# Two transformer layers on one core: transposed rows kept as high and low parts, queries by split operands, another order on three queues

## The chip, the cores and the metric

The kernel runs on one core of a Trainium2 chip. The metric is the device time of one execution in microseconds (us). Before the change the median of three runs is 758.07 us (757.8 to 762.49). The profiled execution, from which every row below is taken, took 760.31 us. A core has five engines that run side by side and meet at semaphores: PE (matrix products), DVE (vector), ACT (activation and copies), POOL (vector work and indirect DMAs) and SP (which only issues DMAs). Each takes its instructions in the order of the program.

## What is computed

Two layers over x of 2 x 2048 rows of 256 words. Cut to what matters:

```python
xn = layernorm(x)
q, k, v = xn@Wq+bq, xn@Wk+bk, xn@Wv+bv         # layer 0, 16 heads of 16
q, k = rope(q), rope(k)
score = einsum('blhd,bmhd->bhlm', q, k)/4       # no softmax
attn = einsum('bhlm,bmhd->blhd', score, v) @ Wo + bo
top_vals, top_idx = top_k(xn @ router_w.T, 2)   # 8 experts, 2 per row
ffn  = sum_k softmax(top_vals)_k * (relu(xn @ w1[e_k])**2 @ w2[e_k])
x = x + attn + ffn
xn = layernorm(x)                               # layer 1
x = x + block_attention(xn) + experts_take_their_512_best_rows(xn)
```

Since layer 0 has no softmax, the kernel computes K^T V once for each batch and multiplies the rotated queries by it.

## The kernel before

**Stage A (pairs of tiles, m = 0 to 15).** A tile is 128 rows, a pair 256. SP loads a pair (`load_pair`, L484), DVE takes its moments, ACT normalises it into `a_xn`, a ring of eight pairs (`normal`, L1265), PE transposes it into a bank of PSUM (`transpose_pair`, L732) and multiplies it by the weights of keys, values and router (`values`, `keys`). The first two pairs are multiplied as plain fp32, the others by split operands: a number is kept as a high part (the type fp32r) and a low part, and a product is high x high + low x high + high x low. ACT writes the high part (`high_xT_pair`), DVE the low one (`low_xT_pair`, L1679), both into buffers of two pairs, and ACT copies the plain transposed pair into `xT_all` as well (`copy_xT_pair`, L1283). DVE finds the two best experts of each row (`top`, `choose`) and, after a count on PE (`rank`), the slot of each row in a table in DRAM, `xs0_d` (`place`).

**Scatters.** POOL carries the rows to their slots: `scatter_x(g, k)` (L2255 to L2268) takes pair g and choice k (0 or 1), writes the number of each row behind it in `a_xn` (an IOTA, L2263) and issues two indirect DMAs (L2266). Pair g has four in all. The second choice overwrites the number, so it waits until the DMAs of the first have landed (`sc0_out`). The order is: first choice of g, second choice of g-1, first choice of g+1 and so on. `normal(m)` waits until all four DMAs of pair m-8 have landed.

**Queries.** `project(g)` (L811, eight groups of four tiles) multiplies `xT_all` by the weights of the queries, 8 instructions of 512 columns in the trace for a group. ACT adds the bias and writes them back over `xT_all` (`copy_q`, L1307), in between it writes the high parts of w2 (`high_w2_0`), DVE the low ones. POOL rotates a tile of queries by a table of cosines and sines (`rotate_q`, L2274), which SP loads (`load_tables`, L551 and L553): the table of tile i waits until tile i-2 has been rotated, since there are two buffers.

**Experts of layer 0.** When every scatter has landed, SP loads tiles of sorted rows (`load_rows`, L543 and L545; a ring of four, so tiles 4 and up wait for the transposes of tile t-4). PE transposes two tiles (`transpose_rows(d)`, L887), multiplies them by w1 (`hidden_pair(d)`, L904) and by w2 (`result0`, L939); a few attention tiles (`attend`) lie between. This repeats 28 times for pairs, then for single tiles. Layer 1 follows and is not touched. SP loads its weights (L529, L535: nine DMAs) right after stage A, while the stage of the queries begins.

What sets the order everywhere is the program as written: there is no scheduler.

## Time and profile before

| | |
|---|---|
| median of 3 runs | 758.07 us (757.8 to 762.49) |
| the profiled execution | 760.31 us |
| its span, first to last instruction | 758.6 us |
| PE busy | 705.8 us, 93% |
| POOL busy | 454.6 us, 60% |
| stage A and queries | 0 to 118.3 us |
| PE idle before the first rows of the experts | 9.5 us |
| experts of layer 0 | 127.8 us on |

"Busy" is the time in which an instruction of the engine runs. A wait is shown in brackets behind the instruction that had waited, with the instruction that released it. A chain follows the work back from the last instruction, each piece to what released it. The granted clock of PE (PEclk) is 1.0 at 2.4 GHz and 0.5 at 1.2 GHz. "Landing" is the time from the issue of a DMA to its semaphore.

### The profile page before, as it was taken

To read this page: it belongs to the slowest core of one execution; us is meant where nothing else is said; L and a number is where in the kernel's file an instruction comes from. 1 tells how busy PE (TensorE), PEld (TensorE's weight loads), DVE (VectorE), ACT (ScalarE), POOL (GpSimd) and SP (SyncE) were. 2 spreads that over 40 slices of the span, in tenths; PEclk is the share of its full clock that TensorE was granted. 3 is DMA by queue.
4 is the path that set the end of the run, shared out by engine and by line. 5 is a ranking of instruction groups with operands and counts; after the bars stand their busy time and mean duration, and the time that the engine had idled before them with its cause. 6 is when DMAs were issued, how large, how long until landed. Compare 5 with 4: busy or idle time off the path is not lost.

```text
span 758.6 us, 19586 instructions
## 1 busy us (share of the span) xinstructions
PE 705.8 (93%) x6224; PEld 631.0 (83%) x6224; DVE 560.0 (74%) x1295; ACT 453.2 (60%) x959; POOL 454.6 (60%) x577
## 2 busy tenths in 40 slices
PE   6999995799999999999998999899999899999994
PEld 4999842799999999999977999777778678888883
DVE  4999771587878888788658886599898777676732
ACT  5666482576776677755525888456677664544411
POOL 3677776799788797988422223034376555655363
PEclk9999997999999999999999999799999999999998
DMA  8699573344445344444178985145457755666352
GB/s 240 183 265 328 185 170 99 90 126 115 129 135 143 104 121 140 130 122 115 41 207 264 313 278 172 30 96 123 109 111 187 223 203 134 148 149 149 50 57 28
DMA packets 151106, 113.99 MB, mean 150 GB/s; under 512 B 59359, under 2 KB 141282, under 8 KB 151012
## 3 DMA queue, kind: packets, MB, share of 16 engines
q1 hardware_dynamic: 137812, 86.94, 41.2%
q0 software_dynamic: 12624, 25.35, 13.4%
q8 instruction: 50, 0.82, 0.5%
q10 hardware_dynamic: 576, 0.53, 0.3%
q14 instruction: 44, 0.36, 0.1%
HBM read 68.68 MB, written 40.80 MB: 144 GB/s over the span
## 4 chain that ended last, share of the span: by engine, by line
PE 85%; DVE 6%; issue 3%; ACT 2%; DMA 1%; POOL 1%; SPq 0%; POOLq 0%; ACTq 0%; DVEq 0%
PE banks L939 13%; PE bank L1195 11%; PE bank L904 11%; PE banks L1206 5%; PE bank L995 5%; PE banks L834 4%; PE bank L915 4%; PE bank L1102 3%; PE banks L770 3%; PE bank L1085 3%; PE banks L823 3%; PE banks L1012 3%; PE bank L776 3%; PE bank L1074 2%; PE bank L887 2%
## 5 line engine op out<-in xcount | busy, mean ns | idle before, releaser
L939 PE MATMUL banks<-r_split,rt_split 128*128 x852 | 110.6, 284 | 1.0 <-issue 0.9
L2297 POOL DMA_INDIRECT ults_by_choice_and_token<-rw,y_id x71 | 79.2, 1115 | 46.5 <-ACT rw L1403 36.3
L939 PEld LDWEIGHTS banks<-r_split,rt_split 128*128 128x128 f32 x852 | 104.9, 191 | 1.6 <-issue 1.6
L904 PE MATMUL bank<-wqkv_split,rt_split 128*128 128x256 f32 x560 | 88.5, 290 | 3.9 <-DVE rt_split L1818 3.8
L1195 PE MATMUL bank<-r_split 128*128 128x512 f32 x384 | 89.6, 391 | 1.3 <-issue 1.1
L1195 PEld LDWEIGHTS bank<-r_split 128*128 128x128 f32 x384 | 71.4, 188 | 16.3 <-issue 1.9
L904 PEld LDWEIGHTS bank<-wqkv_split,rt_split 128*128 128x128 f32 x560 | 77.6, 193 | 5.9 <-DVE rt_split L1818 5.7
L2396 POOL DMA_INDIRECT out_x<-r,idx x32 | 50.2, 1569 | 52.9 <-DVE r L2155 45.2
L2266 POOL DMA_INDIRECT rows_by_expert<-rw,slots x64 | 67.2, 1051 | 18.6 <-issue 9.8
L1818 DVE TENSOR_TENSOR rt_split<-r,rt_split 128x512 fp32r<-128x512 f32 x56 | 59.8, 1108 | 20.0 <-ACT rt_split L1326 20.0
L1843 DVE TENSOR_TENSOR rt_split<-rw,rt_split 128x512 fp32r<-128x512 f32 x71 | 62.9, 918 | 7.4 <-ACT rt_split L1396 7.1
L1581 ACT ACTIVATE r<-bank 128x512 f32<-128x512 f32 x32 | 19.2, 599 | 63.6 <-PE bank L1195 63.6
L2324 POOL TENSOR_TENSOR rw<-rw,bo_s 128x512 f32<-128x512 f32 x16 | 20.6, 1290 | 59.1 <-DVE rw L1892 54.1
L1837 DVE TENSOR_TENSOR rw<-rw 128x512 f32<-128x512 f32 x44 | 42.0, 954 | 18.9 <-ACT rw L1385 18.5
L1385 ACT ACTIVATE rw<-bank 128x512 f32<-128x512 f32 x71 | 41.9, 591 | 20.2 <-PE bank L904 12.0
L1396 ACT ACTIVATE rt_split<-rw 128x512 fp32r<-128x512 f32 x71 | 41.3, 618 | 17.6 <-DVE rw L1837 17.6
L1206 PE MATMUL banks<-r_split 128*128 128x256 f32 x384 | 48.4, 285 | 1.5 <-DVE r_split L2145 0.8
L995 PE MATMUL bank<-rt_split,wqkv_split 128*128 128x256 f32 x384 | 49.2, 283 | 0.3 <-ACT r L1460 0.3
L1206 PEld LDWEIGHTS banks<-r_split 128*128 128x128 f32 x384 | 46.7, 192 | 2.4 <-DVE r_split L2145 1.2
L1326 ACT ACTIVATE rt_split<-r 128x512 fp32r x56 | 32.3, 624 | 25.8 <-PE bank L904 25.6
L995 PEld LDWEIGHTS bank<-rt_split,wqkv_split 128*128 128x128 f32 x384 | 46.3, 188 | 0.8 <-issue 0.7
L2354 POOL DMA_INDIRECT r<-rows_layer,idx x32 | 36.7, 1146 | 14.0 <-issue 13.9
(284 smaller groups left out, 1768.2 us busy)
## 6 DMA issues: line engine op xcount, KB each, us to landing
rt<-in_w SPq DMA_DIRECT2D x24, 512.0 KB, 4.7
rw<-rows_by_expert SPq DMA_DIRECT2D x71, 128.0 KB
r<-in_w SPq DMA_DIRECT2D x16, 512.0 KB
rt<-ults_by_choice_and_token SPq DMA_DIRECT2D x32, 256.0 KB, 3.9
rw<-in_x SPq DMA_DIRECT2D x16, 256.0 KB, 4.7
rw<-in_sin_q SPq DMA_DIRECT2D x32, 128.0 KB
rw<-x_layer SPq DMA_DIRECT2D x16, 256.0 KB
x_plus_bias<-rw SPq DMA_DIRECT2D x16, 256.0 KB, 3.2
```

The lines of the kernel that those rows point to most:

```text
L904: last = pe.matmul(bank[1 + b][:, k * 2 * P:(k + 1) * 2 * P], w[:, c, o:o + P], x[d % 2][:, c, :], start=n == 0, stop=n == 3 * DC - 1)
L939: last = pe.matmul(bank[6 + t % 2][:, 0:D], hidden_T(h, t, c), w[:, ds(e2, 1), o + c * D:o + (c + 1) * D], start=n == 0, stop=n == 3 * HC - 1)
L995: last = pe.matmul(bank[banks[b]][:, j % 2 * D:(j % 2 + 1) * D], w[:, c, j * P:(j + 1) * P], x[:, v.k % 2, c, :], start=k == 0, stop=k == ...
L1195: last = pe.matmul(bank[2 * (hb % 2) + k][:, :], w[:, o:o + P], x[:, s.par, c, :], start=n == 0, stop=n == 3 * DC - 1)
L1206: last = pe.matmul(bank[6 + i % 2][:, 0:D], h[:, s.par, c, i * P:(i + 1) * P], w[s.par][:, o:o + D], start=c == 0 and n == 0, stop=c == HC ...
L1385: act.activation(c_r[:, t % 2, :], bank[1 + t % 2][:, :], ACT.Relu).then_inc(relu_sb, 1)
L1818: dve.tensor_tensor(c_w1lo[:, c, :].unsqueeze(1), r1[:, ds(e1, 1), c * H:(c + 1) * H], c_w1hi[:, c, :].unsqueeze(1).bitcast(F32), ALU.subt ...
L1837: dve.tensor_tensor(c_sq[:, t % 2, :], c_r[:, t % 2, :], c_r[:, t % 2, :], ALU.mult).then_inc(sq_r, 1)
L1843: dve.tensor_tensor(c_lo[:, t % XB, :, :].rearrange("p c n -> p (c n)"), c_sq[:, t % 2, :], c_hi[:, t % XB, :, :].rearrange("p c n -> p (c ...
L2266: pool.indirect_dma_start(xs0_d[:, :], bass.IndirectOffsetOnAxis(slots0_v[:, k, GT * g + j:GT * g + j + 1], 0), a_xn[:, g % NX, j, :], Non ...
L2297: pool.indirect_dma_start(y0_d[:, :], bass.IndirectOffsetOnAxis(y_id[:, t:t + 1].bitcast(I32), 0), c_y[:, t % XB, :], None, bounds_check=l ...
L2396: pool.indirect_dma_start(out[:, :], bass.IndirectOffsetOnAxis(idx1[:, e * TE + i:e * TE + i + 1], 0), f_y[s.par][:, i, :], None, bounds_c ...
```

## The change

It has these parts.

1. **High and low for all pairs.** `xT_all` no longer holds the plain transposed rows. ACT writes the high part of every pair into `xhi_all` (in its place) and DVE the low part into `xlo_all` (the memory of w2's high parts). For the first two pairs ACT makes a plain copy besides (`a_raw`). For 14 pairs ACT has one copy less, for two pairs DVE has one subtraction more.
2. **Queries by split operands.** The weights of the queries are loaded at m = 5 and split by ACT (m = 8) and DVE (m = 9). `project` multiplies high and low parts: 12 instructions of 512 columns for a group. The last group is cut in two: its first half stands ahead of `transpose_rows(0)`, its second behind it.
3. **w2's parts later.** w2's high part e takes the place of `xlo_all`'s group e, so it waits for `project(e)`. One is made after each group, and the last behind the last group. ACT makes w1's high part ahead of the first sorted rows.
4. **Numbers ahead of scatters.** The first eight pairs are numbered by one IOTA at the start. The IOTA of the second choice stands between the two DMAs of the next pair's first choice.
5. **SP's queue.** Behind the last scatter SP loads sorted rows 0 to 3 first, then the tables of tiles 2 and 3, of 4 and 5, and then the weights of layer 1 (they take the place of the queries' split weights, so they wait for `q_ps`), and then sorted rows 4.

```diff
@@ SP
-            sp.wait_ge(k_ps, NPR)
-            for dst, src in ((wqkv1_s[:, :, 0:3 * D], wqkv1.rearrange("(c p) n -> p c n", p=P)),
...
+            def load_late_consts():
+                sp.wait_ge(q_ps, NQ)
+                for dst, src in ((wqkv1_s[:, :, 0:3 * D], wqkv1.rearrange("(c p) n -> p c n", p=P)),
...
             sp.wait_ge(zero_out, 16 * (E + 1))
+            for t in range(XB):
+                load_rows(t)
             for i in range(2, 4):
                 load_tables(i)
                 load_xq(i)
-            for t in range(XB):
-                load_rows(t)
             for i in range(4, QE):
                 load_tables(i)
+            load_late_consts()
@@ PE
+                hi, lo = xhi_all[:, :, g * QT * P:(g + 1) * QT * P], xlo_all[:, g, :, :]
+                for r in parts:
+                    if g >= 2:
+                        pe.wait_ge(q_sb, 2 * (g - 2) + r + 1)
+                    n = 0
                     for c in range(DC):
-                        last = pe.matmul(bank[Q_BANKS[g % 2][r]][:, :], wqkv0_s[:, c, KVR + r * P:KVR + (r + 1) * P],
-                                         xT_all[:, c, g * QT * P:(g + 1) * QT * P], start=c == 0, stop=c == DC - 1)
+                        for w, x in ((wq_hi, hi), (wq_hi, lo), (wq_lo, hi)):
+                            last = pe.matmul(bank[Q_BANKS[g % 2][r]][:, :], w[:, c, r * P:(r + 1) * P], x[:, c, :],
+                                             start=n == 0, stop=n == 3 * DC - 1)
+                            n += 1
...
             for g in range(3, NQ):
+                project(g, range(DC if g < NQ - 1 else 1))
                 if g == NQ - 1:
                     transpose_rows(0)
-                project(g)
+                    project(g, range(1, DC))
@@ ACT
             def high_xT_pair(m):
                 act.wait_ge(aT_ps, 2 * (m + 1))
...
+                if m < NF:
+                    act.activation(a_raw[:, m, :, :], both, ACT.Copy).then_inc(xraw_r, 1)
+                act.activation(xhi_all[:, :, 2 * m * P:2 * (m + 1) * P], both, ACT.Copy).then_inc(aT_sb, 2)
...
+            high_w2_0(E - 2)
+            high_w1(0)
+            high_rows_T(0)
+            copy_q(NQ - 1)
+            high_w2_0(E - 1)
@@ DVE
+            for e in range(E - 1):
+                low_w2_0(e)
+            low_w1(0)
             low_rows_T(0)
-            low_w1(0)
+            low_w2_0(E - 1)
@@ POOL
+            first_ids = number_rows(0, 0, NX)
+            for g in range(NG + 1):
+                if g < NG:
+                    if g >= NX:
+                        pool.wait_ge(sc0_out[g % 4], 16 * TOPK * GT * ((g - NX) // 4 + 1))
+                        first_ids = number_rows(g, 0)
                     pool.wait_ge(slot_r, g + 1)
                     if g >= 4:
                         pool.wait_ge(sc0_out[g % 4], 16 * TOPK * GT * (g // 4))
...
+                    pool.wait_ge(pseq, first_ids)
+                    scatter_x(g, 0, 0)
+                if g >= 1:
+                    h = g - 1
+                    pool.wait_ge(sc0_out[h % 4], 16 * TOPK * GT * (h // 4) + 16 * GT)
+                    second_ids = number_rows(h, 1)
                 if g < NG:
-                    scatter_x(g, 0)
+                    scatter_x(g, 0, 1)
                 if g >= 1:
-                    scatter_x(g - 1, 1)
+                    pool.wait_ge(pseq, second_ids)
+                    for j in range(GT):
+                        scatter_x(h, 1, j)
```

Three places show how the instructions now stand.

POOL, in the middle of the scatters (the DMAs write a table in DRAM, `rows_by_expert`; `rows_scattered` is the semaphore of their landing, `pool_chain` that of the IOTA). Before:

```order
L2263 IOTA rw 128x2 [waits rows_scattered_0]
L2266 DMA rows_by_expert<-rw,slots 66432x257 [waits pool_chain]
L2266 DMA rows_by_expert<-rw,slots 66432x257
L2263 IOTA rw 128x2 [waits slots_ready]
L2266 DMA rows_by_expert<-rw,slots 66432x257 [waits pool_chain]
L2266 DMA rows_by_expert<-rw,slots 66432x257
L2263 IOTA rw 128x2 [waits rows_scattered_1]
```

Now:

```order
L2268 IOTA rw 128x2 [waits rows_scattered_2]
L2275 DMA rows_by_expert<-rw,slots 66432x257
L2275 DMA rows_by_expert<-rw,slots 66432x257 [waits pool_chain]
L2275 DMA rows_by_expert<-rw,slots 66432x257
L2275 DMA rows_by_expert<-rw,slots 66432x257 [waits pool_chain,rows_scattered_0,slots_ready]
L2268 IOTA rw 128x2 [waits rows_scattered_3]
L2275 DMA rows_by_expert<-rw,slots 66432x257
```

The IOTA of the second choice waited with four DMAs between it and the last one that it waits for (two of the pair before, two of the next). Now three stand between: two of the second choice of the pair before, one of the next pair's first. The DMAs behind the IOTA no longer wait for it, save the third.

SP, behind the last scatter (`rows_by_expert` to `rw` and `y_id` are a tile of sorted rows and their numbers, `in_cos_q` and `in_sin_q` the table of a tile of queries; `q_products` counts rotated tiles). Before:

```order
L551 DMA rw<-in_cos_q 128x128 [waits tile_table_ready,rows_scattered_3,zero_rows_stored,rows_scattered_2,q_products,rows_scattered_1,rows_scattered_0]
L553 DMA rw<-in_sin_q 128x2x128
L561 DMA rw<-in_x 128x256
L551 DMA rw<-in_cos_q 128x128 [waits q_products]
L553 DMA rw<-in_sin_q 128x2x128
L561 DMA rw<-in_x 128x256
L542 TENSOR_LOAD tile_r
...
L543 DMA rw<-rows_by_expert 128x256
...
L545 DMA y_id<-rows_by_expert 128x1
L542 TENSOR_LOAD tile_r
```

Now:

```order
L551 DMA rw<-rows_by_expert 128x256
...
L553 DMA y_id<-rows_by_expert 128x1
L559 DMA rw<-in_cos_q 128x128 [waits q_products]
L561 DMA rw<-in_sin_q 128x2x128
L569 DMA rw<-in_x 128x256
...
L559 DMA rw<-in_cos_q 128x128 [waits q_products]
...
L559 DMA rw<-in_cos_q 128x128 [waits q_products]
...
L538 DMA wqkv<-in_wqkv 128x2x768 [waits q_in_psum]
L538 DMA wo_s<-in_wo 128x2x256
...
L544 DMA bv_c<-in_bv 32x2x1 x4
L550 TENSOR_LOAD tile_r [waits rows_loaded_0,rows_T_in_psum]
```

The tables of tiles 2 and 3 stood ahead of the sorted rows and now stand behind them; the nine loads of layer 1's weights (`in_wqkv` to `in_bv`), which stood ahead of the very first tables, now stand between the table of tile 5 and sorted rows 4 (the last row).

PE, around the first sorted rows (`ident,rw` are the transposes of sorted rows; `512`-column products are the queries, `bank` and `banks` their halves). Before:

```order
L887 MATMUL bank<-ident,rw 128x128 [waits ktv_masked,rows_loaded_1,rows_loaded_0]
L887 MATMUL bank<-ident,rw 128x128 x3
L823 MATMUL bank<-r,wqkv 128x512 [waits q_ready]
L823 MATMUL bank<-r,wqkv 128x512
L823 MATMUL banks<-r,wqkv 128x512 x2
L887 MATMUL bank<-ident,rw 128x128 [waits q_ready,rows_loaded_3,rows_loaded_2]
L887 MATMUL bank<-ident,rw 128x128 x3
L904 MATMUL bank<-wqkv_split,rt_split 128x256 [waits rows_T_low_ready,w1_copied,m_ready]
L904 MATMUL bank<-rw_split,rt_split 128x256
```

Now:

```order
L831 MATMUL bank<-r_split,wqkv_split 128x512 [waits q_ready]
L831 MATMUL bank<-r_split,wqkv_split 128x512
L831 MATMUL bank<-r_split,wq_high_or_w_low_split 128x512
...
L897 MATMUL bank<-ident,rw 128x128 [waits ktv_masked,rows_loaded_1,rows_loaded_0]
L897 MATMUL bank<-ident,rw 128x128 x3
L831 MATMUL banks<-r_split,wqkv_split 128x512 [waits q_ready]
L831 MATMUL banks<-r_split,wqkv_split 128x512
L831 MATMUL banks<-r_split,wq_high_or_w_low_split 128x512
...
L897 MATMUL bank<-ident,rw 128x128 [waits q_ready,rows_loaded_3,rows_loaded_2]
L897 MATMUL bank<-ident,rw 128x128 x3
L914 MATMUL bank<-wq_high_or_w_low_split,rt_split 128x256 [waits rows_T_low_ready,w1_copied,m_ready]
```

Half of the last group of queries has moved ahead of the first transposes, and its products read parts instead of plain words.

## Rows read from the trace of the kernel before

**Rows 1.** The page's first lines: the span; busy time, share and instructions of each engine.

```profile
span 758.6 us, 19586 instructions
...
PE 705.8 (93%) x6224; PEld 631.0 (83%) x6224; DVE 560.0 (74%) x1295; ACT 453.2 (60%) x959; POOL 454.6 (60%) x577
```

**Rows 2.** Windows: busy us (instructions) of each engine, PEclk, DMA share, GB/s.

```profile
128.00:130.00 2.00, 2.00 (x6) 1.33 (x6) 0.47 (x1) 0.95 (x2) 0.00 (x0) 0.50 0.37 85
...
142.00:144.00 2.00, 2.00 (x13) 2.00 (x12) 2.00 (x3) 1.11 (x2) 1.96 (x2) 0.58 0.19 55
```

**Rows 3.** Chain that ended last, in order of time: start us, us, what.

```profile
90.60 3.54 PE banks L823 x8
...
127.78 1.09 PE bank L887 x4
128.87 3.38 PE bank L823 x4
132.25 1.73 PE banks L823 x4
...
136.04 2.86 PE bank L904 x24
...
141.70 4.64 PE bank L904 x24
...
150.07 0.44 PE bank L887 x4
```

**Rows 4.** Timeline of POOL: start us, us, what, [idle before <-releaser].

```profile
54.30 0.97 POOL L2266 DMA_INDIRECT rows_by_expert<-rw,slots  x1 [0.30 <-issue]
55.29 0.15 POOL L2263 IOTA rw<- 128x2 int32 x1
55.71 0.99 POOL L2266 DMA_INDIRECT rows_by_expert<-rw,slots  x1 [0.28 <-POOL rw L2263]
...
61.77 0.13 POOL L2263 IOTA rw<- 128x2 int32 x1 [1.08 <-DMA rows_by_expert<-rw,slots]
...
116.04 0.97 POOL L2266 DMA_INDIRECT rows_by_expert<-rw,slots  x1 [0.30 <-issue]
```

**Rows 5.** Waits of POOL from 20 to 118 us: in total, times, longest.

```profile
POOL rw L2263 <- DMA rows_by_expert<-rw,slots: 4.0, 5, 1.5
```

**Rows 6.** DMA issues by line, 20 to 40 us; last number: median us to landing.

```profile
rows_by_expert<-rw,slots POOLq DMA_INDIRECT x13, 3.1
```

**Rows 7.** The same from 40 to 60 us.

```profile
rows_by_expert<-rw,slots POOLq DMA_INDIRECT x16, 6.7
```

**Rows 8.** The same from 80 to 100 us.

```profile
rows_by_expert<-rw,slots POOLq DMA_INDIRECT x15, 3.4
```

**Rows 9.** Timeline of POOL after the scatters: rotation of queries, a scatter of results.

```profile
133.01 0.46 POOL L2283 TENSOR_TENSOR rw<-r,rw 128x128 f32<-128x128 f32 x1 [5.18 <-DMA rw<-in_sin_q]
...
156.22 1.26 POOL L2297 DMA_INDIRECT ults_by_choice_and_token<-rw,y_id  x1 [0.15 <-issue]
```

**Rows 10.** Timeline of SP's queue, constants of layer 1.

```profile
88.49 0.37 SPq L529 DMA_DIRECT2D wqkv<-in_wqkv  x1
...
91.17 1.95 SPq L535 DMA_DIRECT2D bv_c<-in_bv  x4
```

**Rows 11.** Timeline of SP's queue behind the last scatter.

```profile
118.81 0.34 SPq L551 DMA_DIRECT2D rw<-in_cos_q  x1
...
123.76 0.36 SPq L543 DMA_DIRECT2D rw<-rows_by_expert  x1
...
125.93 0.33 SPq L545 DMA_DIRECT2D y_id<-rows_by_expert  x1
...
130.01 0.57 SPq L553 DMA_DIRECT2D rw<-in_sin_q  x1
```

**Rows 12.** Timeline of ACT: normalisation of the last pair.

```profile
77.08 1.10 ACT L1265 ACTIVATE rw<-rw,rt 128x256 f32<-128x256 f32 x2
```

**Rows 13.** Chain near the end: split operands, 512 columns.

```profile
706.15 5.92 PE bank L1195 x26
```

More of the change, by code:

```diff
@@ L50 @@
 NG = NT // GT
+QT = 4
+NF = 2
 SPAN = 2 * NT
@@ L809, in rank, with project @@
                 last.then_inc(rank_ps, 1)
-            def project(g):
-                if g >= 2:
-                    pe.wait_ge(q_sb, 2 * (g - 1))
+            def project(g, parts=range(DC)):
                 if g == 0:
-                    pe.wait_ge(consts_q, 16 * 4)
+                    pe.wait_ge(wkv_r, 4)
                     pe.wait_ge(v_sb, NPR)
@@ L1354, in _ @@
                     act.activation(wkv_hi, wkv_raw, ACT.Copy).then_inc(wkv_r, 1)
+                if m == 8:
+                    act.wait_ge(consts, 16 * 3)
+                    act.activation(wq_hi, wq_raw, ACT.Copy).then_inc(wkv_r, 1)
                 if m + 2 < NPR:
@@ L1759, in _ @@
                     place(m - 2)
-                if NF <= m < NPR:
+                if m < NPR:
                     low_xT_pair(m)
@@ L1764, in _ @@
                     choose(m - 1)
+                if m == 9:
+                    dve.wait_ge(wkv_r, 3)
+                    dve.tensor_tensor(wq_lo, wq_raw, wq_hi.bitcast(F32), ALU.subtract).then_inc(wkv_r, 1)
                 if m >= 2:
@@ L1805, in _ @@
             dve.tensor_tensor(top_v[:, :, 2], top_v[:, :, 1], top_v[:, :, 0], ALU.subtract).then_inc(top_de, 1)
-            for e in range(E):
-                low_w2_0(e)
             dve.wait_ge(top_de, 2)
```

123 lines of the change are left out of this document (55 added, 68 removed).

## The prediction

> **What bounds the kernel now.** The first lines of the page come first: PE is busy for 93% of the span [rows 1], so what PE waits for, or what it stops doing, decides. The reader then looks for the stretches in which PE does not work. In the part that the change touches there is one: the chain that ended last runs through PE up to the queries, and then PE stands until the first sorted rows are transposed, at 127.78. The idle time is 9.5 us, and behind it PE runs at half clock: four products of the last group of queries take 3.38 us and the next four 1.73 [rows 3], while the granted clock reads 0.50 [rows 2].
>
> What PE waits for there is POOL and then SP. POOL issues the last scatter at 116.04 [rows 4], it lands, and at 118.81 SP issues its first DMA behind it [rows 11]. I call this moment R. SP first issues six DMAs of tables and x, then the sorted rows: tile 0 at 123.76, the last of tile 1 at 125.93, and 1.85 us later PE transposes them [rows 3, 11]. So the end of the scatters and SP's queue set the start of the experts, and the speed of the queries' products does not. In the experts PE is again the bound.
>
> I therefore ask two things: when does R come, and how long after R does PE get into step. As a mark for the second I take the transposes of the fourth couple of sorted tiles (6 and 7): before at 150.07, R + 31.3 [rows 3].
>
> **When R comes: the scatters.** A DMA of POOL takes 0.97 to 0.99, with 0.30 between two of them; the IOTA takes 0.15 and the DMA behind it starts 0.28 later [rows 4]. A pair has four DMAs and two IOTAs: 3.92 + 0.60 + 0.86 = 5.4 us, and 16 pairs make most of the 96 us of scatters.
>
> The change hides IOTAs. An IOTA that no DMA waits for lies inside the gap that a DMA has anyway: a DMA of POOL behind a vector instruction that it does not wait for started 0.15 later [rows 9], and 0.15 + 0.15 is the gap of 0.30. So a pair takes 3.92 + 4 x 0.30 = 5.1 in the first eight pairs. From pair 8 on the first choice's IOTA still stands right ahead of the DMA that waits for it, which leaves 5.25. The gain is about 7 x 0.32 + 8 x 0.19 = 3.8 us. Its bounds are 1.2 (eight IOTAs of 0.15, if the gap behind an IOTA stays) and 9 (if the 0.28 behind all 32 went to nothing).
>
> Against it stands the landing. The second choice's IOTA had four DMAs between it and the last one that it waits for, and now has three. Counted from that DMA's start, a landing is now noticed from 0.98 + 3 x 1.3 = 4.9 us on, where it was 6.4. And it has become a loop: the DMA that the next IOTA waits for stands right behind this one, so a pair can't take less than a landing and 0.3. The median landing was 3.1 us at 20 to 40, 6.7 at 40 to 60 and 3.4 at 80 to 100 [rows 6 to 8]; one from 54.30 was waited for until 61.77, 7.4 us [rows 4]. The old order hid nearly all of this: five waits, 4.0 us in all, at most 1.5 [rows 5]. In the new one a pair with a landing of 7.0 takes 7.3 and not 5.1. The landings are long while SP's loads of weights share the DMA engines, for some seven pairs, and for two more near the end, when zero rows are stored.
>
> What it costs depends on whether a landing gets shorter when POOL has fewer DMAs out. If not, nine pairs pay about 2.1: 19 us. If it shrinks with the number in flight, from five to four, 7.0 becomes 5.6, a pair takes 5.9, and nine pay 0.8: 7 us. Nothing is the lower bound. I take 1.05 for each of the nine, 9.5 us, nearer to the second: only five pairs had to wait before, so the others landed sooner than 6.4, and the stores of the zero rows no longer meet the weights of layer 1. R moves by 9.5 - 3.8 - 4.0 (the old waits) = +1.7 us. Its range is -8 to +11.
>
> The Trainium skill, "DMA: Bandwidth & Descriptors" (section "Anatomy of one DMA — SWDGE (gpsimd) path"), gives such a DMA 2.0 us and its bytes over 436 GB/s. For 131.6 KB that is an estimate of 2.3 us, by which no IOTA would ever wait, and R would move by -7.8. The shortest medians are not far from it, the loaded ones are three times as long; the same page (section "Queues, rings and completion order") has the engines take turns between queues in whole packets, which fits. The trace decides for the long landings.
>
> **From R to the mark.** SP now issues sorted tiles 0 to 3 first. The six DMAs ahead of them took 118.81 to 123.76, of which the reading of a tile's number, some 0.8, stays [rows 11]. Tiles 0 and 1 are transposed at about R + 4.8, not + 9.0. Then come six products of the last group of queries (before eight, 5.1 us [rows 3]), at half clock 2.7 us, ACT's two copies, the second transposes, and the first products with w1 from R + 10.5, not + 17.2. They end at R + 13.5. This is the gain that one would expect, 6.7 us.
>
> But PE then needs tiles 4 and 5, and SP's queue has this ahead of them. Four tiles at 1.6 us each (tile 0 to the last of tile 1: 2.17 us, of which 0.5 lies inside a tile [rows 11]) end at R + 6.5. Six DMAs of tables and x, at 0.7 each, end at + 9.9. The table of tile 4 waits until POOL has multiplied tile 2, whose table, with its sine DMA at + 7.0, lands 3.0 later (130.01 to 133.01 [rows 9, 11]); four multiplications at 0.42 make + 11.7. The table of tile 5 waits for tile 3 in the same way, + 14.5, and is out at + 15.7. Now the nine loads of layer 1's weights, 88.49 to 93.12, 4.6 us of SP's time [rows 10]: + 20.4. Behind them tile 4 at + 21.2, the last DMA of tile 5 at + 23.4, and 1.85 later, at R + 25.2, PE may transpose. It has stood for over 11 us, more than before the first rows, and is at half clock again.
>
> Before, the transposes of tiles 4 and 5 did not wait, and the second products with w1 began at R + 22.9, after a wait for w1's low part. From there to the mark it took 8.4 us, with the first products at half clock as well (4.64 where the pair before took 2.86 [rows 2, 3]). Now that wait is covered: transposes 1.1, and 8.4 again, gives R + 34.7. So PE gets into step 3.4 us later than before, counted from R. The lower bound is 2.6, where tile 7 (two more tables ahead of it in SP's queue, the second waiting for a rotation) lands at + 33.9; the upper one 5, with the results at half clock too. Behind the mark nothing differs: PE is the bound, and POOL's rotations, late by up to 7 us at tile 6, have caught up at tile 8.
>
> **What costs nothing.** The queries' products become 12 x 0.228 = 2.7 us a group (split operands, 26 in 5.92 [rows 13]) where eight took 3.54 [rows 3]: 0.8 less, eight times, all of it in the stretch in which PE waits for the scatters; without that cover it would be worth 6.5. w2's parts are spread over the groups, which ACT and DVE finish before R + 4.8. The copy that ACT saves in 14 pairs lies beside PE. The additional copies of the first two pairs delay the first slots by less than one copy (two of 256 words take 1.10 [rows 12]); it is inside the range of R. If the scatters fall far behind, ACT's normalisation of the last pair, at 77.08 [rows 12], waits for those of pair 7; that delays stage A, which ends well before R.
>
> **The sum.** +1.7 + 3.4 = +5.1 us. It is made against the profiled execution, whose span is 758.6; the median lies at 758.07, 0.5 below that span, so I forecast 763.2 for the median.
>
> **The rivals.**
> - Slower by much: the landings stay as long as they were. R moves by 19 - 7.8 = +11, the sum is +14.6, 772.7 us. For it speaks that SP's loads fill the engines whatever POOL does, against it the short landings outside of them. It decides from a mean cost of 1.35 for the nine pairs, above which the whole is over 1% slower.
> - The scatters gain in full: no IOTA waits, R moves by -7.8 and the sum is -4.4, 753.7 us. The medians of 3.1 and 3.4 speak for it, 6.7 against it.
> - The early rows keep their lead: PE is not held for tiles 4 and 5, since the tables come back faster or the nine loads cost SP little. Then the mark comes 6.7 us earlier than before, and the whole takes 753.1 with my R and 743.6 with the full gain of the scatters. The order of SP's queue speaks against it: the waits on rotated tiles stand in it.
> - The change doesn't do what it says: IOTAs stay visible (gain 1.2), and landings take it back; this is the first rival's direction, about 766.
>
> **Chances.** About a measurement's resolution is 1%, 7.6 us: faster is below 750.5, slower above 765.7. My forecast 0.46, full gain of the scatters 0.18, landings unchanged 0.16, visible IOTAs 0.06, early rows keep their lead 0.14. Faster takes most of the last, 0.10. Slower takes the landings, half of the visible IOTAs and the part of the forecast in which R moves by over 4 us, 0.27. The rest, 0.63, is within 1%. The range goes from 752.5, below the full gain, to 772.5.
>
> **What would show it.** In the changed profile: POOL's IOTAs waiting for `rows_by_expert` between 36 and 75 us, in most pairs, with 10 us in all; the last scatter between 114 and 122 us; first transposes some 5 us behind it and not 9; then a wait of PE of over 10 us ahead of the third transposes, with SP's nine loads just before. I am wrong if the third transposes follow without a wait, or if the IOTAs wait for 15 us or for none.

## The result, and the profile after

The changed kernel took 768.05 us (median of four runs, 765.29 to 769.04), the kernel before beside it 758.03. The ratio is 1.0109, with an interval of [1.0078, 1.014]: slower, by just over 1%. I had forecast 763.2, and had given 0.27 to a time above 765.7. The profiled execution took 767.43 us.

The head of its page, which answers to [rows 1]:

```profile
span 765.7 us, 19610 instructions
...
PE   703.3 (92%) x6256; PEld 639.8 (84%) x6256; DVE 563.7 (74%) x1298; ACT 449.1 (59%) x948; POOL 455.9 (60%) x570
```

The span grew by 7.1 us, although PE is busy 2.5 us less. So PE stands for longer. The waits of PE from 10 to 180 us (engine, line, releaser: us in all, times, longest):

```profile
PE bank L897 <- issue: 19.2, 2, 11.1
...
PE bank L897 <- ACT r L1313: 1.4, 1, 1.4
```

L897 is the transposes of the sorted rows. Before, they waited once for rows, 9.5 us; now they wait twice, 8.1 and 11.1. (The 1.4 us for ACT was there before too.) The timeline of PE (start, duration, instruction, idle time before it in brackets) shows where, against [rows 3]:

```profile
125.04 1.08 PE L897 MATMUL bank<-ident,rw 128*128 128x128 f32 x4 [8.12 <-issue]
...
130.13 1.09 PE L897 MATMUL bank<-ident,rw 128*128 128x128 f32 x4 [1.45 <-ACT r L1313]
...
146.44 1.09 PE L897 MATMUL bank<-ident,rw 128*128 128x128 f32 x4 [11.11 <-issue]
147.18 4.82 PE L914 MATMUL bank<-wq_high_or_w_low_split,rt_split 128*128 128x256 f32 x24
...
155.56 0.60 PE L897 MATMUL bank<-ident,rw 128*128 128x128 f32 x4
```

The first transposes come 2.7 us earlier than before, the second ones 5.3 us earlier, the third 7.7 us later and the fourth, the mark, 5.65 us later. PE is at half clock again for the products behind the wait. The windows of this stretch (length, busy time of PE, PEld, DVE, ACT, POOL, granted clock, DMA share, GB/s), beside [rows 2]:

```profile
120.00:130.00 10.00, 3.64 (x10) 2.57 (x10) 2.84 (x4) 1.87 (x4) 5.61 (x9) 0.52 0.34 90
130.00:140.00 10.00, 5.20 (x28) 5.03 (x28) 6.47 (x8) 4.91 (x8) 9.28 (x14) 0.67 0.37 109
140.00:150.00 10.00, 3.56 (x17) 3.59 (x18) 1.55 (x2) 0.60 (x1) 6.23 (x13) 0.50 0.55 158
```

Why PE had no rows is in SP's own queue, which answers to [rows 11]:

```profile
121.03 0.37 SPq L551 DMA_DIRECT2D rw<-rows_by_expert  x1
...
126.44 0.33 SPq L553 DMA_DIRECT2D y_id<-rows_by_expert  x1
...
132.96 0.33 SPq L559 DMA_DIRECT2D rw<-in_cos_q  x1
...
137.06 0.60 SPq L538 DMA_DIRECT2D wqkv<-in_wqkv  x1
...
139.71 1.84 SPq L544 DMA_DIRECT2D bv_c<-in_bv  x4
142.38 0.37 SPq L551 DMA_DIRECT2D rw<-rows_by_expert  x1
...
144.65 0.33 SPq L553 DMA_DIRECT2D y_id<-rows_by_expert  x1
```

Rows 0 to 3 are out by 126.8. Then come the tables of tiles 2 and 3, those of 4 and 5 at 132.96 and 136.09, and the nine loads of layer 1's weights, 137.06 to 141.55. Only then come rows 4 and 5. The last DMA of row 5 goes out at 144.65, and 1.8 us later PE transposes.

POOL's waits from 20 to 130 us, which answer to [rows 5], and one pair of scatters from its timeline, which answer to [rows 4]:

```profile
POOL rows_by_expert L2275 <- issue: 13.1, 47, 0.3
POOL rows_by_expert L2275 <- DVE slots L1727: 12.7, 2, 10.5
POOL rows_by_expert L2275 <- POOL rw L2268: 7.8, 15, 0.8
POOL rw L2268 <- DMA rows_by_expert<-rw,slots: 6.0, 6, 2.8
```

```profile
85.31 0.15 POOL L2268 IOTA rw<- 128x2 int32 x1
86.28 0.99 POOL L2275 DMA_INDIRECT rows_by_expert<-rw,slots  x1 [0.81 <-POOL rw L2268]
87.29 0.15 POOL L2268 IOTA rw<- 128x2 int32 x1
87.61 1.00 POOL L2275 DMA_INDIRECT rows_by_expert<-rw,slots  x1 [0.18 <-issue]
...
91.24 0.16 POOL L2268 IOTA rw<- 128x2 int32 x1
```

The IOTA at 87.29 (the second choice's) is hidden as expected: 0.18 us behind it the next DMA starts. Behind the one at 85.31 (the first choice's) the gap is 0.81 us, where before it was 0.28. A pair takes 5.9 us, not the 5.4 of before.

### The profile page after: what moved, and what is told of

Its sections match the earlier page's. It is cut to its first block, busy times and chain, and to the rows that moved or that the text cites. A ratio compares the mean times of both kernels' runs of the same rounds, so it can differ in the third digit from the quotient of the medians.

```text
span 765.7 us, 19610 instructions
## 1 busy us (share of the span) xinstructions
PE 703.3 (92%) x6256; PEld 639.8 (84%) x6256; DVE 563.7 (74%) x1298; ACT 449.1 (59%) x948; POOL 455.9 (60%) x570
## 4 chain that ended last, share of the span: by engine, by line
PE 64%; POOL 11%; issue 7%; DMA 7%; DVE 5%; SPq 3%; ACT 1%; POOLq 0%; DVEq 0%; ACTq 0%
PE bank L1206 11%; PE banks L949 10%; PE bank L914 8%; POOL rows_by_expert L2275 6%; PE banks L1217 5%; PE bank L1006 5%; DMA rows_by_expert<-rw,slots 5%; PE banks L844 4%; PE bank L925 3%; PE bank L1113 3%; PE bank L1096 3%; PE banks L1023 3%; PE bank L1085 2%; PE bank L897 1%; PE banks L1070 1%
## 5 line engine op out<-in xcount | busy, mean ns | idle before, releaser
L914 PE MATMUL bank<-wq_high_or_w_low_split,rt_split 128*128 128x256 f32 x560 | 90.0, 293 | 1.5 <-DVE rt_split L1825 1.3
L2275 POOL DMA_INDIRECT rows_by_expert<-rw,slots x64 | 65.5, 1024 | 33.7 <-issue 13.1
L914 PEld LDWEIGHTS bank<-wq_high_or_w_low_split,rt_split 128*128 128x128 f32 x560 | 79.0, 196 | 2.9 <-DVE rt_split L1825 2.6
L1844 DVE TENSOR_TENSOR rw<-rw 128x512 f32<-128x512 f32 x44 | 40.5, 920 | 21.0 <-ACT rw L1393 20.5
L1006 PE MATMUL bank<-rt_split,wq_high_or_w_low_split 128*128 128x256 f32 x256 | 47.3, 285 | 0.3 <-ACT r L1468 0.3
L897 PE MATMUL bank<-ident,rw 128*128 128x128 f32 x142 | 24.1, 286 | 22.6 <-issue 21.1
```

Of the source, the lines that this page charges most:

```text
L914: last = pe.matmul(bank[1 + b][:, k * 2 * P:(k + 1) * 2 * P], w[:, c, o:o + P], x[d % 2][:, c, :], start=n == 0, stop=n == 3 * DC - 1)
L1006: last = pe.matmul(bank[banks[b]][:, j % 2 * D:(j % 2 + 1) * D], w[:, c, j * P:(j + 1) * P], x[:, v.k % 2, c, :], start=k == 0, stop=k == ...
L2275: pool.indirect_dma_start(xs0_d[:, :], bass.IndirectOffsetOnAxis(slots0_v[:, k, GT * g + j:GT * g + j + 1], 0), a_xn[:, g % NX, j, :], Non ...
```

## The experiments

None of the twelve ran under the conditions of the first measurement. Runs e0 to e7 were on one chip (number 0) and e9 to e12 on another (number 13), and on both the kernel before takes 785 to 787 us, not 758. The number of the chip of the first measurement is not on record; I call it the first chip. In every profile of the later chips ACT waits for something that the trace puts outside the core; the two profiles of the first chip have no such row. The two largest rows of the changed kernel itself (e0), from 0 to 200 us (four rows, 41 us in all):

```profile
ACT r_split L1284 <- remote: 17.1, 4, 6.3
ACT rt L1296 <- remote: 16.4, 4, 5.1
```

What ACT waits for there stays open. With it the last scatter comes some 15 us later, POOL waits 20 to 43 us for slots instead of 13, and when the scatters have landed PE often still has queries to do. SP is also released later behind the last scatter: 3.2 to 9.7 us, where both kernels needed 2.8 on the first chip. So a time on these chips says less about R. What they do show are distances in a queue. As R I take the moment when SP is released (0.75 us ahead of its first DMA where that is a sorted row, whose number it reads first): 118.81 before, 120.28 after. In the table "row 5" is the last DMA of sorted row 5, "third" the third transposes, "mark" the fourth, each in us behind R, from the timeline of one profile per kernel (that of e1 is of an execution of 791.04 us, and e1's median is 785.18). Each ratio is to the kernel before, run beside it on the same chip.

| kernel | ratio to before | interval | row 5 | third | wait of PE before third | mark |
|---|---|---|---|---|---|---|
| before (first chip) | 1 | | 16.1 | 19.9 | 0 | 31.1 |
| changed (first chip) | 1.0109 | 1.0078 to 1.014 | 24.4 | 26.2 | 11.1 | 35.3 |
| e0_after_again | 1.0028 | 0.9998 to 1.0059 | 26.4 | 28.2 | 5.5 | 36.9 |
| e1_scatter_only | 0.9956 | 0.9916 to 0.9997 | 19.0 | 22.4 | 0 | 33.4 |
| e2_rows_first_only | 1.0031 | 0.9996 to 1.0066 | 18.4 | 20.7 | 0 | 32.0 |
| e3_weights_later | 0.9996 | 0.9962 to 1.0031 | 19.0 | 24.5 | 0 | 34.2 |
| e4_old_scatters | 1.0062 | 1.0023 to 1.0101 | 27.0 | 29.0 | 0 | 39.9 |
| e5_waits_before_iota | 1.0045 | 1.002 to 1.0071 | 25.3 | 27.1 | 0 | 38.0 |
| e6_tables_behind_rows | 1.0025 | 0.9987 to 1.0063 | 16.2 | 24.1 | 0 | 35.3 |
| e7_high_part_only | 1.0014 | 0.9984 to 1.0045 | 25.0 | 26.9 | 9.2 | 35.5 |
| e9_parts_alone | 1.0009 | 0.9985 to 1.0032 | 22.5 | 24.3 | 0 | 34.0 |
| e10_all_but_parts | 0.9982 | 0.9955 to 1.001 | 19.1 | 20.9 | 2.9 | 31.6 |
| e11_tables_later | 1.0046 | 1.0023 to 1.0069 | 13.7 | 18.9 | 0 | 34.3 |
| e12_second_choice_two_behind | 1.0075 | 1.004 to 1.0111 | 13.6 | 15.7 | 0 | 32.8 |

### One part at a time

`e1_scatter_only` is the kernel before with the new order of scatters (part 4 of the change), `e2_rows_first_only` the kernel before with sorted rows 0 to 3 ahead of the tables of tiles 2 and 3 (the first half of part 5), `e4_old_scatters` the changed kernel with the old scatters.

The edit of e1, and with plus and minus exchanged that of e4 (both with the new or old `scatter_x`, as in the diff of the change):

```diff
-                    scatter_x(g, 0)
+                    pool.wait_ge(pseq, first_ids)
+                    scatter_x(g, 0, 0)
                 if g >= 1:
-                    scatter_x(g - 1, 1)
+                    h = g - 1
+                    pool.wait_ge(sc0_out[h % 4], 16 * TOPK * GT * (h // 4) + 16 * GT)
+                    second_ids = number_rows(h, 1)
...
+                    for j in range(GT):
+                        scatter_x(h, 1, j)
```

The edit of e2:

```diff
+            for t in range(XB):
+                load_rows(t)
             for i in range(2, 4):
                 load_tables(i)
                 load_xq(i)
-            for t in range(XB):
-                load_rows(t)
```

> The kernel before with the changed order of numbers and scatters alone. Theory (the loss comes mostly from SP's queue): the last scatter starts at 117.5 and not at 116.0, everything behind it keeps its distances, 759.5 us. Rival (the loss comes from the scatters, and the rest hides behind them): the whole +5.6 us at the mark appears here already, 763.7 us. In both the DMA behind the IOTA of pairs 8 and up starts 0.8 us later, where before it was 0.28.

> The kernel before with sorted rows 0 to 3 loaded ahead of the tables of tiles 2 and 3, the weights of layer 1 left where they were (early). Theory: the first transposes come 4.2 us earlier, the third ones at R + 20.5 (held by the tables that wait for rotations, without the 4.6 us of the nine loads), the mark (transposes of tiles 6 and 7) at R + 30, 1.3 us earlier than before: 756.7 us. Rival (sorted rows first are a gain that lasts): 4 to 6 us faster, 752 to 754.

> The changed kernel with the old order of numbers and scatters (four DMAs between the last one waited for and the IOTA). Theory: R comes at 118.8 plus at most 0.3, some 1.5 us earlier, 766.5 us; IOTAs wait for landings 4 us in all, not 6. Rival (the scatters are what costs): 762.5 us.

These expectations were in absolute times against 758, and the chip was another, so only ratios and distances can be read. The ratios are worth -3.5 us for the scatters, +2.4 for the rows, +4.9 for the change without its scatters. None of the three came as the theory said. e1 was to be 1.4 us or more slower and is faster. e2 was to be 1.3 us faster: its third transposes came where expected (R + 20.7 for 20.5), its mark did not (32.0 for 30). e4 was to be faster than the changed kernel, by either theory, and is slower; its IOTAs wait 2.6 us for landings, not 4. Later runs filled in the other combinations: `e10_all_but_parts` has scatters and rows, `e9_parts_alone` only the split parts (1, 2, 3 and the late loads that they force), with tables and x of tiles 2 and 3 ahead of the rows.

> The kernel before with the other two parts of the change, the scatters in the new order and sorted rows 0 to 3 ahead of the tables of tiles 2 and 3, but x^T kept once and queries by eight plain products. Layer 1's weights are then loaded in the old place, ahead of the scatters' end. Theory: no wait of PE above 5 us ahead of the third transposes, the mark at R + 29 to 32, and the whole 1 to 5 us under before (the scatters alone gave a ratio of 0.9956, the rows alone 1.0031). Rival: the two together cost what the changed kernel costs, and the whole lies at or above the changed kernel's ratio of 1.0028.

> The split parts alone: rows kept as high and low parts, queries by split operands and what that forces (w2's high parts one per group of queries, layer 1's nine loads behind the last group), with the old scatters and the tables and x of tiles 2 and 3 ahead of the sorted rows. Theory: this part carries the cost of the change, by two ways: SP's queue ahead of row 4 and ACT's and DVE's work on w2's parts among the last queries. It is 5 to 8 us over the kernel before of the same call (where the scatters are not the bound, the products moved behind the last slots count too), and the second transposes wait for ACT by 2.8 us and not 1.45. Rival: the split parts cost nothing by themselves and the order of rows and tables carries it; then within 2 us of before.

> The changed kernel itself, beside the kernel before on the chip of this call, so that the others can be read against both. The four variants of the first call stood on a chip on which the first part of the program took some 15 us longer (scatters waiting for slots), so distances are counted from R, the first DMA of SP behind the last scatter. My theory: first transposes at R + 4 to 6 unless PE is still busy with queries, third transposes at R + 24 to 26, the mark (fourth transposes) at R + 34 to 36, R itself 1.5 us later than before if the scatters are the bound and no later if slots are; the whole 7 to 10 us over before. Rival, in which the 10 us come from R alone (landings): the mark at R + 31 as before and R 7 us or more later.

e0 was to cost 7 to 10 us over before and costs 2.2. Its third transposes (28.2) and its mark (36.9) come later than the 24 to 26 and 34 to 36 expected, since PE was still busy with queries: its first transposes are at R + 12.1.

So seven of the eight combinations have a ratio, and each part can be read three times, by what its addition changes:

| part | alone | with one other | with two others | mean |
|---|---|---|---|---|
| scatters | -0.44% | -0.49% (to rows) | -0.34% (to rows and split parts) | -0.42%, -3.3 us |
| rows first | +0.31% | +0.26% (to scatters), +0.53% (to split parts) | | +0.37%, +2.9 us |
| split parts | +0.09% | +0.31% (to rows) | +0.46% (to rows and scatters) | +0.29%, +2.3 us |

A single difference is about as large as its uncertainty (0.2 to 0.6 points), but the three of a part have one sign. The three share runs and stem from two chips, so they are not independent; from the intervals I estimate a mean to be uncertain by about 0.25 points, and 0.29 is hardly clear of that. On these chips the new order of the scatters gains, and rows first and, less surely, the split parts cost. Why the scatters gain here, where POOL waits mostly for slots, is not shown. By the ratios e9, which was to be 5 to 8 us over before, is 0.7 over, so that theory fell: on these chips the split parts alone do not carry the change's cost. e10 was to be 1 to 5 under and is 1.4 under, with an interval that holds 1. That the second transposes wait 2.8 us for ACT in e9, and not 1.45, came true; it is the work on w2's and w1's high parts in ACT's queue ahead of the last queries' copies.

### What holds row 5

`e7_high_part_only` takes away two thirds of the queries' products, 64 of 96.

```diff
-                        for w, x in ((wq_hi, hi), (wq_hi, lo), (wq_lo, hi)):
+                        for w, x in ((wq_hi, hi),):
...
-                                             start=n == 0, stop=n == 3 * DC - 1)
+                                             start=n == 0, stop=n == DC - 1)
```

> The change, leaving out two of three products of each query group (only high part times high part, 4 products of 12 per group and half; the queries are less exact). It takes 16 products of 0.23 us, 3.7 us, off each of eight groups, 29 us of PE's work. Theory: this work lies in the time in which PE waits for the scatters, so the first transposes stay at R + 4 to 6, the mark at R + 34 to 36, and the whole within 2 us of the changed kernel (more where the first part is not bound by the scatters; and PE, idle for longer, may run at half clock a little earlier). Rival: the queries' products bind, and the whole falls by 10 us or more.

The expectation counted this wrongly: a group loses 8 products and not 16, so 64 at 0.23 us are some 15 us of work, not 29 (PE's busy time fell by 10.5 us, with more of it at half clock). The median is 1 us above that of the changed kernel of the same chip, and the mark is at R + 35.5, as expected. PE stands instead. Its timeline at the first three transposes:

```profile
143.41 0.60 PE L897 MATMUL bank<-ident,rw 128*128 128x128 f32 x4
...
150.19 1.08 PE L897 MATMUL bank<-ident,rw 128*128 128x128 f32 x4 [5.71 <-ACT r L1313]
...
165.29 1.09 PE L897 MATMUL bank<-ident,rw 128*128 128x128 f32 x4 [9.22 <-issue]
```

SP's queue of the same run:

```profile
155.80 0.60 SPq L538 DMA_DIRECT2D wqkv<-in_wqkv  x1
...
158.46 1.84 SPq L544 DMA_DIRECT2D bv_c<-in_bv  x4
161.13 0.37 SPq L551 DMA_DIRECT2D rw<-rows_by_expert  x1
...
163.40 0.33 SPq L553 DMA_DIRECT2D y_id<-rows_by_expert  x1
```

This is the picture of the first chip: PE, which has come to the experts in time, waits 9.2 us for rows that stand behind the nine loads. The third transposes are at R + 26.9; the changed kernel has 26.2 on the first chip and 28.2 on this one.

`e3_weights_later` spreads the nine loads over rows 8 to 16. `e6_tables_behind_rows` does that and puts the tables of tiles 4 and 5 behind row 5. The places in SP's order that e6 changes (e3 has the first added pair of lines and keeps the tables):

```diff
-            for i in range(4, QE):
-                load_tables(i)
-            load_late_consts()
...
+                if 8 <= t < 17:
+                    load_late_const(t - 8)
+                if t == XB + 1:
+                    load_tables(4)
+                    load_tables(5)
```

> The changed kernel with the nine loads of layer 1's weights one by one among the sorted rows 8 to 16 and not ahead of row 4. Theory: the third transposes come 4.6 us earlier and so does all behind them: 763.4 us. Rival (the tables' waits for rotations, or the landing of the scatters, is what costs): no change within 1 us, 767 to 769.

> The change with another order in SP's queue: the tables of query tiles 4 and 5 (which wait for rotations) stand behind sorted rows 4 and 5, and the nine loads of layer 1's weights are spread one by one over the loads of rows 8 to 16. Theory: third transposes at R + 14 to 16 and not + 25, no wait of PE above 5 us ahead of them, the mark at R + 25 to 28, and the whole 7 to 10 us under the changed kernel of the same call, 0 to 3 us under before. Rival: PE in its stead waits for something else there (w1's parts, POOL's rotations), and the mark stays at R + 33 or later, the whole within 2 us of the changed kernel.

The column "row 5" is the direct answer: 24.4 to 27.0 us with the nine loads and the tables ahead of it (22.5 in e9, where rows 0 to 3 go behind the first tables), 19.0 with the tables alone, 16.2 with neither (then it is the ring of four that holds row 4 until the first transposes, here at R + 12.6). In neither kernel does PE wait for rows 4 and 5. Beside e0, e3 has its third transposes 3.8 us earlier (4.6 were expected) and its mark 2.7; its ratio is lower by 0.32 points, within the noise of the two. And e6 does not gain: its mark is at R + 35.3 and the whole equals the changed kernel. I had expected 25 to 28. That is the chip: the first transposes come at R + 12.6 because PE is still busy, so there was little lead to keep, and from there PE goes its own pace. It waits 2.8 us for ACT ahead of the second transposes, runs the first products with w1 at half clock (5.4 us and not 2.9), and waits for DVE's low part of w1 ahead of the second, as the kernel before does:

```profile
161.48 4.63 PE L919 MATMUL bank<-wq_high_or_w_low_split,rt_split 128*128 128x256 f32 x24 [2.40 <-DVE rt_split L1830]
```

The mark then follows without a wait. It could not have come much earlier, though: the last DMA of row 7 is at R + 32.4, which the next run shows to be the next limit.

`e11_tables_later` makes the same move of the tables in the kernel before, with rows 0 to 3 first; it has neither split parts nor late loads. `e12_second_choice_two_behind` adds another order of the scatters:

```diff
-                    h = g - 1
+                h = g - LAG
...
+                    scatter_x(h, 1, 0)
+                if NX <= g + 1 < NG:
+                    pool.wait_ge(sc0_out[(g + 1) % 4], 16 * TOPK * GT * ((g + 1 - NX) // 4 + 1))
+                    ids[g + 1] = number_rows(g + 1, 0)
+                if h >= 0:
+                    scatter_x(h, 1, 1)
```

> The kernel before, with sorted rows 0 to 3 ahead of the tables and the tables of query tiles 4 and 5 behind rows 4 and 5; scatters and x^T as before. If SP's order is what keeps PE from rows 4 and 5 it starts as early as it can here: the third transposes follow the second by what PE has to do, as before, and the early rows keep their lead. Theory: the mark at R + 25 to 28 where PE waits for R, and 2 to 5 us under before; where PE still has queries to do when R comes, as in the runs of this chip so far, there is little to gain: within 2 us. Rival: POOL's rotations of tiles 4 and 5, now later, hold the attention's products of those tiles, and it is slower by 2 us or more.

> As the run with the tables later, and the scatters of the second choice two pairs behind those of the first, so that seven DMAs of POOL and not three or four lie between a row's number being written and the landing that it waits for; the first choice's IOTA is issued a DMA ahead. Theory: no IOTA waits for a landing (under 1 us in all), a pair takes 5.1 to 5.3 us, and R comes 2 to 5 us earlier than in the run with the tables later, unless slots bind; then no difference. The whole 2 to 6 us under before: this is the version that should beat both. Rival: more rows in flight make each landing longer and the waits for the landing of four pairs back take it back.

In e11 row 5 is out at R + 13.7 and the third transposes follow the second without a wait, but then PE waits ahead of the mark:

```profile
164.69 1.03 PE L835 MATMUL banks<-m_all,r 128*128 128x256 f32 x4
171.03 1.09 PE L888 MATMUL bank<-ident,rw 128*128 128x128 f32 x4 [5.32 <-issue]
```

and SP's queue gives the reason:

```profile
157.19 0.55 SPq L553 DMA_DIRECT2D rw<-in_sin_q  x1
...
161.88 0.55 SPq L553 DMA_DIRECT2D rw<-in_sin_q  x1
163.25 0.36 SPq L543 DMA_DIRECT2D rw<-rows_by_expert  x1
...
168.68 0.34 SPq L543 DMA_DIRECT2D rw<-rows_by_expert  x1
169.20 0.33 SPq L545 DMA_DIRECT2D y_id<-rows_by_expert  x1
```

Row 6, at 163.25, and row 7, at 168.68, stand behind the tables of the tiles that follow, each of which waits for a rotation. The wait was not removed, only moved by one couple. The last DMA of row 7 is at R + 32.4 in e11; before it was at R + 25.4. In e12 PE waits 6.1 us at the same place. e11 was to be within 2 us of before and is 3.6 us slower, e12 was to be 2 to 6 us faster and is 5.9 us slower; the mark is at R + 34.3 and 32.8. A table moved behind a row later meets another row. Whether this wait is all of the cost was not separated.

### The gap of 0.81 us

`e5_waits_before_iota` takes the waits for slots and landings ahead of the first choice's IOTA, from pair 8 on.

```diff
                 if g < NG:
-                    if g >= NX:
-                        pool.wait_ge(sc0_out[g % 4], 16 * TOPK * GT * ((g - NX) // 4 + 1))
-                        first_ids = number_rows(g, 0)
...
+                    if g >= NX:
+                        first_ids = number_rows(g, 0)
                     pool.wait_ge(pseq, first_ids)
```

> The change, but from pair 8 on POOL waits for the pair's slots and for the landing of the pair four back ahead of the first IOTA, not behind it, so that its DMA waits for the IOTA alone. In the changed kernel that DMA stood 0.81 us behind the IOTA and not 0.28. Theory: the 0.81 comes from the three waits that POOL takes between the IOTA and the DMA; here the gap reads 0.28, a pair of four DMAs 5.4 us and not 5.9, and R comes about 4 us earlier than in the changed kernel where the scatters are the bound (nothing where slots are). Rival: the gap belongs to the place in the order and stays 0.8; then R and the whole stay.

```profile
93.65 0.13 POOL L2268 IOTA rw<- 128x2 int32 x1
94.06 0.99 POOL L2275 DMA_INDIRECT rows_by_expert<-rw,slots  x1 [0.28 <-issue]
95.07 0.15 POOL L2268 IOTA rw<- 128x2 int32 x1
95.39 1.00 POOL L2275 DMA_INDIRECT rows_by_expert<-rw,slots  x1 [0.18 <-issue]
```

The gap is 0.28 again and a pair without a wait takes 5.3 us and not 5.9, as the first theory said: what stands between the IOTA and its DMA costs 0.5 us, though nothing was waited for. Slots bind on this chip (12.7 us of slot waits have moved ahead of the IOTAs). The last scatter went out 2.0 us earlier than in e0 (131.45, 133.50), but SP was released 6.8 us behind it and not 3.3, so R came 1.5 us later, and the ratio, 1.0045, is no better than that of the changed kernel. What it would give on the first chip was not measured.

In e12 no IOTA waits for a landing, as expected. The waits of POOL from 20 to 140 us:

```profile
POOL rows_by_expert L2266 <- DVE slots L1722: 43.2, 12, 10.6
```

No row of a landing is left, but the slots take it all: the last scatter goes out at 132.98, in e11 at 131.86. And R comes 9.7 us behind it (4.9 in e11). The last thing that SP waits for there is a store of zero rows into the same table; in the chain that ended last (start, duration) it reads:

```profile
134.98 7.64 DMA rows_by_expert<-rw
```

It lands at 142.62. In e12 SP issues layer 1's weights from 121.9, then tables and x, and only then the zero rows, and from 130 to 140 us the DMA engines are busy for 0.99 of the time (0.42 in e11). In the kernel before on the first chip all of this was issued by 103 us, 13 us ahead of the last scatter. No variant beat both kernels by more than its interval except e1, which is under before by 0.03 to 0.84%.

## Why the prediction was right, and where it was off

**From R to the mark: right in mechanism and size.** The term was +3.4 (2.6 to 5). In the chain of waits (0.17 us behind the timeline's start that the table above shows) the mark is at 155.73, R + 35.45, against R + 31.26 before: +4.2. Step by step, predicted and measured behind R: first transposes 4.8 and 4.8; table of tile 4 11.7 and 12.7; of tile 5 14.5 and 15.8; the nine loads 4.6 and 4.5 us; last DMA of tile 5 23.4 and 24.4; third transposes 25.2 and 26.2; wait of PE over 11 and 11.1; mark 34.7 and 35.45. One step went otherwise and cost nothing: the first products with w1 began half at half clock and ended at R + 15.1, not 13.5, inside the wait. (The sum has "six DMAs at 0.7 each" from + 6.5 to + 9.9; they are 0.57 each, and its end was right.) The one microsecond that is missing up to the third transposes arises in one place, POOL's first rotation behind R:

```profile
130.22 0.46 POOL L2308 TENSOR_TENSOR rw<-r,rw 128x128 f32<-128x128 f32 x1 [4.29 <-DMA rw<-in_sin_q]
...
131.05 1.46 POOL L2308 TENSOR_TENSOR rw<-r,rw 128x128 f32<-128x128 f32 x1
```

The third multiplication takes 1.46 us and not 0.46. DVE runs this meanwhile, the subtraction for w2's low part, which the change has moved there:

```profile
130.97 1.23 DVE L1743 TENSOR_TENSOR r_split<-r,r_split 128x1024 fp32r<-128x1024 f32 x1 [3.48 <-ACT r_split L1306]
```

The Trainium skill, "SBUF — State Buffer" (section "Who interferes with whom"), says that a DVE instruction with two inputs in SBUF contends with a POOL instruction that reads SBUF, that their shared port pair is an exclusive lock, and that the order of issue decides who is held. DVE started first here, at 130.97. If POOL has to wait for its end at 132.20, the multiplication ends about 0.4 us behind it, near 132.6; it ended at 132.51, and the trace agrees.

**R: the sum was right by luck, both its parts were wrong.** Predicted +1.7 (-8 to +11), measured +1.5. From the start of the first to that of the last scatter POOL took 95.4 us before (20.63 to 116.04) and 97.5 after (20.05 to 117.54), and it started 0.6 us earlier. Adding up all rows of its timeline between them:

| | before | after | change | predicted |
|---|---|---|---|---|
| IOTAs and the gaps of DMAs and IOTAs | 23.4 | 24.7 | +1.4 | -3.8 |
| waits for landings | 4.0 | 6.0 | +2.1 | +5.5 |
| the DMAs themselves | 66.2 | 64.5 | -1.7 | 0 |
| waits for slots | 1.9 | 2.2 | +0.3 | 0 |

The step that failed is "From pair 8 on the first choice's IOTA still stands right ahead of the DMA that waits for it, which leaves 5.25." A pair takes 5.9 there, since the gap behind the IOTA grew from 0.28 to 0.81. I had counted the instructions and not the waits that now stand between them. In the first eight pairs the step nearly held: the gap behind a hidden IOTA is 0.17 to 0.18, and a pair without a wait takes 5.2 us. (The sum itself was loose: the terms as printed, 5.38 against 5.12 and 5.25, give a gain of 2.9 and not 3.8.) And the landings cost less than I took, 0.7 us for each of nine pairs in place of 1.05, nearer still to the lower bound. The sign that I had named, IOTAs waiting in most pairs and for 10 us in all, did not come: six wait, 6.0 us in all, 4.8 of it in two of them. The two errors of 5.2 and -3.4, with the DMAs' -1.7 and the earlier start, cancel. I had not forecast that -1.7: before, three of the DMAs behind 100 us took 1.8 to 1.95 us, after, one, and why is open. The range of this term was wide for the second and did not hold the first: its gain was bounded at 1.2 to 9, and it was a loss.

Whether a landing gets shorter with fewer DMAs in flight, the question between the bounds, stays open. At 40 to 60 us the median is 5.6, and 6.7 before [rows 7], the five to four that I had supposed; but the DMA engines were less busy there too (a share of 0.87, 0.94 before). In the three other stretches it did not fall: 4.6 for 3.1 at 20 to 40 us, 6.2 for 5.2 at 60 to 80, 3.6 for 3.4 at 80 to 100. The row of after for 40 to 60 us:

```profile
DMA to landing us min/median/max: 4.0/5.6/8.3
```

**The queries cost nothing: right.** On the first chip PE waits 8.1 us behind them; e7, without two thirds of them, is not faster on a chip on which they are less covered. It moves the first transposes from R + 12.1 to R + 5.0, and the nine loads and the tables take the lead back.

**"Behind the mark nothing differs": off by 1.4 us.** The transposes of the sorted rows stay 5.65 to 5.8 us late up to the eighteenth couple, then 5.4 to 7.0, at the end 6.35; the whole span is 7.1 longer. The largest single wait among these transposes is one of 1.2 us, at the 24th. No run separated it.

**The median.** The profiled executions differ by 7.1 us, the medians by 10.0. I set the sum against the median by the span (758.6 and 758.07). The profiled execution of before had itself taken 760.31, 2.2 us over its median, and that of after 0.6 under its own. That makes the difference of 2.9. The miss, 768.05 for 763.2, is 4.9 us: these 2.9, and 2.0 by which the profiled difference of 7.1 exceeds the sum of 5.1 (0.8 from R to the mark, 1.4 behind it, less 0.2 for R). It is inside the range of 752.5 to 772.5. Of the four rivals the one nearest in time was that of the visible IOTAs, 766 with a chance of 0.06: IOTAs did become dearer, but its landings did not.

**What stays open.** Where the chips differ, so does the price of the change: 1.0109 on the first, 1.0028 on the one of e0. On the first the wait before the third transposes was whole (11.1 us), in e0 half (5.5), since PE arrived later. That the rest of the difference comes from this is argued, not shown; no single part ran on the first chip.

## What to carry to other kernels

When a load is moved ahead in a queue, write down the whole queue up to the next item that the bound engine needs, not only up to the item that was moved. The gain of the first rows (5.3 us) was lost on the next ones (7.7 us) because unrelated loads, and waits of another engine, stood between, and moving them again (e11) only moved the wait. And in a loop of small instructions a wait has a price of its own: order them so that what is already fulfilled stands ahead of the instruction on which the next depends. In e5 this took 0.5 us off a pair; that it shortens the whole was not shown.

## What the runs showed of the hardware

- An indirect DMA of POOL starts 0.30 us behind another one, 0.17 to 0.18 behind an IOTA that it does not depend on, 0.28 behind one that it waits for, and 0.81 where two more waits, long fulfilled, stand between. Moving these waits ahead of the IOTA gave 0.28 again (e5).
- A multiplication of POOL of 0.46 us takes 1.46 beside a subtraction of DVE of 1.23 us that started just ahead of it and has both inputs in SBUF.
- The same kernel before took 758 us in the first measurement and 785 to 787 us on both chips of the later runs, where ACT waits for something outside the core (41 us in e0), which the first profiles do not show. The ratio of the change was 1.0109 (1.0078 to 1.014) there and 1.0028 (0.9998 to 1.0059) in e0, so a small change has to be measured where it is to be used.
- A store of zero rows landed 7.64 us after its issue where the DMA engines were busy for 0.99 of the stretch from 130 to 140 us (e12).
